# Two experts on each side of a convolution, run batch by batch, with the convolution's tiles put between the expert steps

## The chip, the cores and the metric

The kernel runs on one core of a Trainium2 chip. The metric is the device time of one execution in microseconds (us). The kernel before takes 614.93 us, the median of three runs (614.17 to 615.29). The engines are TensorE (PE in the rows, with its weight loads as PEld), VectorE (DVE), ScalarE (ACT), GpSimd (POOL) and SyncE (SP), whose queue issues all the DMAs here.

## The reference

The input x has 2 batches, 8 channels and 256 x 256 values. Four residual layers follow, each on a group-normalised input. Layers 0, 2 and 3 are expert layers, in which every channel has its own two-layer network. Layer 1 is a 3x3 convolution over all 8 channels, with binarised weights and copied edges.

```python
# _gn: mean and variance over 2 channels x 256 x 256, for each batch and each of 4 groups
x = x + _L0_conv_ref(_gn(x), ...)   # expert: h = gelu(x @ w1[e] + b1[e]); out = h @ w2[e] + b2[e]
x = x + _L1_conv_ref(_gn(x), weight, bias)   # conv 3x3, 8 -> 8 channels, weights sign(w) * mean|w|
x = x + _L2_conv_ref(_gn(x), ...)   # expert, as L0
x = x + _L3_conv_ref(_gn(x), ...)   # expert, exact gelu
```

w1 is 8 x 256 x 1024 and w2 is 8 x 1024 x 256, so an expert is 256 -> 1024 -> 256 for 2 x 256 tokens.

## The kernel before, in words

The 24 experts are numbered E0 to E23; E0 to E7 are layer 0, E8 to E15 layer 2, E16 to E23 layer 3. The convolution stands between E7 and E8.

**An expert step.** Every product is made of three matmuls (low part of the weights by high part of the data, high by low, high by high). One of the 8 steps t of an expert makes 128 of its 1024 hidden values: `g1` (L1004) issues 6 matmuls into a bank G1, ScalarE applies gelu and makes the high part (`gelu`, L559 and L563), VectorE subtracts for the low part (`h_lo`, L720), and two steps later `g2` (L1020) issues 6 matmuls that add to the two ACC banks. After the last step VectorE adds ACC, bias and residual into XT (`evict`, L734). A step is 512 columns wide when both batches run together. An expert in `HALVED` (E7, E8, E9) runs as two passes of 8 steps of 256 columns, one for each batch; E8 and E9 run in the order E8 batch 0, E9 batch 0, E8 batch 1, E9 batch 1. Beside the steps, ScalarE and VectorE split the next expert's weights into high and low parts (`w_hi`, `w_lo`, one of 8 pieces a step), and normalise and split its input (`norm`, `x_hi`, `x_lo`).

**The group statistics.** A job J is a chain over engines: `sums` (two bn_stats, VectorE), `aggregate`, `mean_over_partitions` (TensorE), `deviate`, `variance_over_partitions` (TensorE), `add_eps`, `rstd` (GpSimd), `scale_shift`. Then `norm`, `x_hi` and `x_lo` make an expert's input from it.

**The convolution.** XT has image rows on the partitions of each channel. The convolution wants all 8 channels of 16 rows on the partitions (XC), so each finished channel is stored to a DRAM scratch (`store_x1`) and loaded again (`load_xc`). A batch is 19 blocks of rows, in 10 tiles: nine of 512 columns and one of 256. Of each tile q, GpSimd normalises (`normalise_tile`, CN), ScalarE makes the high part Ch (L617), VectorE the low part Cl (`conv_low`, L894), TensorE issues 3 matmuls by Ch and 3 by Cl (L1122), ScalarE scales and adds the bias in the bank (L622), and VectorE adds into XC (`conv_add`, L903). Then `give_back` (L436) issues 20 DMAs a batch that bring XC back to XT. The semaphore `x2_in[b]` counts them.

**What sets the order.** Each engine's program is written out by hand and waits in order on semaphores. In the kernel before, TensorE finishes E7 (`drain`), then runs all 20 tiles, then E8. VectorE does the sums of batch 0 for E8 (job 9) after `conv_low` of tile 17, behind a wait for all 20 DMAs of batch 0:

```python
            conv_low(q - 3)
            dve.wait_ge(x2_in[0], 16 * pieces_back())
            sums(9, 0)
            sums_done(9)
            aggregate(9)
            conv_add(q - 5)
```

Of the kernel before, what the change touches and what calls it, by code (L numbers as in the profile page):

```python
# [108 lines left out]
def evicts_for(E, b, layer):


    if not isinstance(E, int):
# [5 lines left out]
    return evicts(E) - DC if E == C + 2 else evicts(E - 1)

ONE_BATCH = {7: 0, 8: 1, 9: 0, 10: 1}


def batches(J):

    return (ONE_BATCH[J],) if isinstance(J, int) and J in ONE_BATCH else tuple(range(B))


def jobs_weighed(J, late):

    return B * J - sum(J > j for j in ONE_BATCH) if isinstance(J, int) else B * J - (len(ONE_BATCH) if late else 0)

USUAL = dict(sums=0, aggregate=1, mean=3, deviate=3, variance=5, eps=6, scale=7)


def jobs_of(P, ee, f):


    if not isinstance(P, int):
        if f == 0:
            return [(2 * P + ee, USUAL, 2 * P - 2 if ee else 2 * P + 2, P - 1 if ee else NPAIR)]  # L150
        return [] if ee else [(P + 7, USUAL, 2 * (P - NPAIR * f) + 2, NPAIR)]
    E = 2 * P + ee
    if E == 0:
        return [(1, dict(sums=4, aggregate=5, mean=7, deviate=7), 2, NPAIR)]
    if E == 1:
        return [(1, dict(variance=0, eps=0, scale=1), 2, NPAIR)]
    if E == 7:
        return [(6, dict(sums=0, aggregate=1, mean=4, deviate=4, variance=6, eps=7, scale=8), 4, 2),
                (7, dict(sums=10, aggregate=11, mean=12, deviate=12, variance=13, eps=13, scale=14), 6, 3)]
    if E == C:  # L160
        return [(11, dict(mean=9, deviate=9, variance=11, eps=11, scale=12), 2, NPAIR)]
    if E == C + 1:
        return [(10, dict(sums=0, aggregate=0, mean=2, deviate=2, variance=3, eps=4, scale=4), 0, NPAIR),
                (11, dict(sums=5, more_sums=6, aggregate=7), 2, NPAIR)]
    if P >= 5 and ee == 0 and P + 1 < LAYERS * NPAIR:
        return [(P + 7, USUAL, (2 * P + 2) % C, NPAIR)]
    return []
# [29 lines left out]
def split_at(P, ee, t):

    E = 2 * P + ee
    if isinstance(P, int):  # L200
        if E == LAYERS * C - 1:
            return None
        if E == C:
            return t + 4 if t < 4 else None
        if E == C + 1:
            return t - HT if t >= HT else None
    return t if t < HT else None
# [955 lines left out]
```

## Time and profile before

| What | Value |
|---|---|
| median of three runs | 614.93 us |
| the profiled execution's own time | 614.43 us |
| its span, first to last instruction | 612.4 us |
| TensorE busy | 594.5 us (97%) |
| ScalarE busy | 430.3 us (70%) |
| VectorE busy | 423.2 us (69%) |
| GpSimd busy | 31.3 us (5%) |
| mean granted TensorE clock | 0.989 |

The rows further down come from this one execution. Times in them count from the span's start; the execution's own time is 2.0 us above the span. A busy TensorE is not TensorE at its peak, since matmuls overlap: the distance between the starts of two rows says more than the duration in one.

### The profile page before, as it was taken

How to read it: one execution, taken by the hardware profiler on the slowest of the kernel's cores; microseconds unless marked ns; L12 is line 12 of the kernel's file. 1: busy time of each engine (PE TensorE's matmuls, PEld its weight loads, DVE VectorE, ACT ScalarE, POOL GpSimd, SP SyncE). 2: the span in 40 equal slices, each digit the busy share in tenths (PEclk: the TensorE clock that was granted, in tenths of full speed). 3: DMA queues.
4: the chain of work that ended last, by engine and by line, in shares of the span. 5: the costliest groups of instructions: out<-in, count | busy, mean ns of one | idle time of the engine just before them, and what ended most of it. 6: DMA issues, size and time to landing. Idle time of an engine off the chain costs nothing.

```text
span 612.4 us, 9520 instructions
## 1 busy us (share of the span) xinstructions
PE 594.5 (97%) x2973; PEld 501.0 (82%) x2973; DVE 423.2 (69%) x857; ACT 430.3 (70%) x741; POOL 31.3 (5%) x52
## 2 busy tenths in 40 slices
PE   7999999999999896999999999999999999999997
PEld 7778888888889775999888888888888888888885
DVE  4867968768787796767865866866775675675532
ACT  5766767677777685769867777777767777777743
POOL 2000000000000451000000000000000000000000
PEclk9999999999999997999999999999999999999999
DMA  8673355455363599801332323223234244234001
GB/s 273 188 238 105 113 163 176 119 165 152 108 178 103 197 116 110 177 2 63 109 105 77 130 68 118 88 74 133 70 109 132 86 123 136 86 116 142 17 19 69
DMA packets 56342, 72.80 MB, mean 119 GB/s; under 512 B 4064, under 2 KB 50160, under 8 KB 56304
## 3 DMA queue, kind: packets, MB, share of 16 engines
q1 hardware_dynamic: 56304, 72.33, 41.5%
q8 instruction: 19, 0.31, 0.2%
q14 instruction: 19, 0.16, 0.1%
HBM read 59.70 MB, written 8.42 MB: 111 GB/s over the span
## 4 chain that ended last, share of the span: by engine, by line
PE 87%; DVE 4%; DMA 2%; issue 2%; SPq 2%; POOL 1%; ACT 1%; DVEq 0%; POOLq 0%; ACTq 0%
PE G L1016 42%; PE ACC L1039 14%; PE ACC L1034 14%; PE ACC L1035 14%; DMA W2raw<-in_L_conv_w 1%; DVE Cl L894 1%; DMA XT<-XC 1%; PE TR L1052 1%; SPq L374 1%; DVE XC L903 1%; DVE BN L653 1%; SPq L436 1%; PE ACC L1122 1%; PE TR L982 1%; PE STAT L995 0%
## 5 line engine op out<-in xcount | busy, mean ns | idle before, releaser
L720 DVE TENSOR_TENSOR Hl<-HR,Hh 128x512 fp32r<-128x512 f32 (+1 forms) x216 | 136.2, 631 | 158.8 <-ACT Hh L563 157.5
L559 ACT ACTIVATE HR<-G,BT 128x512 f32<-128x512 f32 (+1 forms) x216 | 138.3, 640 | 137.1 <-PE G L1016 135.9
L1016 PE MATMUL G<-Xh,W1l 128*128 128x512 f32 (+1 forms) x432 | 163.9, 379 | 3.3 <-issue 1.9
L1016 PE MATMUL G<-Xl,W1h 128*128 128x512 f32 (+1 forms) x432 | 158.7, 367 | 0.0
L1016 PE MATMUL G<-Xh,W1h 128*128 128x512 f32 (+1 forms) x432 | 158.5, 367 | 0.0
L1034 PE MATMUL ACC<-Hh,W2l 128*128 128x512 f32 (+1 forms) x432 | 156.5, 367 | 0.0
L1035 PE MATMUL ACC<-Hh,W2h 128*128 128x512 f32 (+1 forms) x432 | 156.2, 366 | 0.0
L563 ACT ACTIVATE Hh<-HR 128x512 fp32r<-128x512 f32 (+1 forms) x216 | 126.3, 585 | 8.7
L1039 PE MATMUL ACC<-Hl,W2h 128*128 128x512 f32 (+1 forms) x432 | 123.5, 367 | 0.6 <-DVE Hl L720 0.6
L1016 PEld LDWEIGHTS G<-Xh,W1l 128*128 128x128 f32 x432 | 82.0, 190 | 16.1 <-issue 2.2
L1016 PEld LDWEIGHTS G<-Xh,W1h 128*128 128x128 f32 x432 | 81.9, 189 | 13.6
L1034 PEld LDWEIGHTS ACC<-Hh,W2l 128*128 128x128 f32 x432 | 81.8, 189 | 13.4
L1035 PEld LDWEIGHTS ACC<-Hh,W2h 128*128 128x128 f32 x432 | 81.8, 189 | 13.2
L1016 PEld LDWEIGHTS G<-Xl,W1h 128*128 128x128 f32 x432 | 82.1, 190 | 11.5
L1039 PEld LDWEIGHTS ACC<-Hl,W2h 128*128 128x128 f32 x432 | 78.2, 189 | 14.5 <-DVE Hl L720 1.3
L699 DVE TENSOR_TENSOR W2l<-W2raw,W2h 128x512 fp32r<-128x512 f32 x96 | 65.6, 686 | 4.2 <-ACT W2h L546 3.6
L699 DVE TENSOR_TENSOR W1l<-W1raw,W1h 128x512 fp32r<-128x512 f32 x96 | 65.5, 686 | 2.7 <-ACT W1h L546 2.5
L546 ACT ACTIVATE W2h<-W2raw 128x512 fp32r<-128x512 f32 x96 | 58.9, 616 | 3.6 <-DMA W2raw<-in_L_conv_w 3.6
L546 ACT ACTIVATE W1h<-W1raw 128x512 fp32r<-128x512 f32 x96 | 58.6, 617 | 2.1 <-DMA W1raw<-in_L_conv_w 2.1
L653 DVE BATCH_NORM_STATS2 BN<-XT 128x6 f32<-128x512 f32 (+1 forms) x60 | 37.3, 680 | 3.2 <-DMA XT<-XC 3.2
L493 POOL TENSOR_TENSOR RS<-VE,half 128x2 f32<-128x2 f32 (+1 forms) x18 | 12.8, 708 | 489.4 <-DVE VE L677 489.4
L714 DVE TENSOR_TENSOR Xl<-XN,Xh 128x512 fp32r<-128x512 f32 x48 | 32.9, 686 | 0.6 <-ACT Xh L553 0.4
(73 smaller groups left out, 357.4 us busy)
## 6 DMA issues: line engine op xcount, KB each, us to landing
W1raw<-in_L_conv_w SPq DMA_DIRECT2D x24, 1024.0 KB, 5.1
W2raw<-in_L_conv_w SPq DMA_DIRECT2D x24, 1024.0 KB, 5.6
x_scratch<-XT SPq DMA_DIRECT2D x16, 256.0 KB
out_x<-OUTT SPq DMA_DIRECT2D x16, 256.0 KB, 2.2
XC<-x_scratch SPq DMA_DIRECT2D x16, 252.0 KB
XT<-XC SPq DMA_DIRECT2D x34, 112.0 KB
NAT<-in_x SPq DMA_DIRECT2D x6, 512.0 KB, 8.4
NAT<-in_x SPq DMA_DIRECT2D x4, 256.0 KB, 3.6
```

Of the source, the lines that this page charges most:

```text
L493: nc.gpsimd.tensor_tensor(RS[:, bs], VE[:, bs], half[:, bs], ALU.pow).then_inc(rs_done, 1)
L546: nc.scalar.activation(dst, src, ACT.Copy).then_inc(whi, 1)
L559: nc.scalar.activation(HR[:, t % 2, 0:n], G1[t % 2][:, 0:n], func, bias=BT[:, bass.ds(col, 1)]).then_inc(gelu_done, 1)
L563: nc.scalar.activation(Hh[:, t % RING, 0:n], HR[:, t % 2, 0:n], ACT.Copy).then_inc(hhi, 1)
L653: nc.vector.bn_stats(BN[:, b, i], at).then_inc(bn_done, 1)
L699: nc.vector.tensor_tensor(dst, src, high.bitcast(F32), ALU.subtract).then_inc(wlo, 1)
L714: nc.vector.tensor_tensor(Xl[:, par, :, b], XN[:, b], Xh[:, par, :, b].bitcast(F32), ALU.subtract).then_inc(xlo, 1)
L720: nc.vector.tensor_tensor(Hl[:, t % RING, 0:n], HR[:, t % 2, 0:n], Hh[:, t % RING, 0:n].bitcast(F32), ALU.subtract).then_inc(hlo, 1)
L1016: ins = nc.tensor.matmul(G1[t % 2][:, 0:width(b)], w[:, ee, c, col], rhs, start=n == 0, stop=n == len(parts) - 1)
L1034: nc.tensor.matmul(banks[m][:, 0:n], W2l[:, ee, t8, col], high, start=t8 == 0, stop=False)
L1035: nc.tensor.matmul(banks[m][:, 0:n], W2h[:, ee, t8, col], high, start=False, stop=False)
L1039: ins = nc.tensor.matmul(banks[m][:, 0:n], W2h[:, ee, t8, col], Hl[:, t % RING, 0:n], start=False, stop=t8 == HT - 1)
```

## The change

The experts that run batch by batch are now E6, E7, E8 and E9, `CROSSED`, in the order of a list of passes. P6 to P9 are E6 batch 0, E7 batch 0, E6 batch 1, E7 batch 1; P10 to P13 are E8 batch 0, E9 batch 0, E8 batch 1, E9 batch 1. A unit u is a step t of a pass, and tables say at which unit everything stands. The tiles of the convolution of batch 0 (0 to 9) stand in TensorE's program from P8 step 7 to P9 step 4, those of batch 1 (10 to 19) from P10 step 4 to P11 step 1. TensorE finishes P9 before it begins P10, and P11 before P12. The loops are written out, HR has 4 buffers in place of 2 and lies under Hl, CN lies under Cl with 3 buffers, and the copied edges of XC (`double_edges`) move from VectorE to GpSimd. In a tile, ScalarE no longer scales the bank: it adds the bias to XC, and VectorE's `conv_add` multiplies the bank by the mean weight and adds.

```diff
-HALVED = (C - 1, C, C + 1)
-CROSSED = (C, C + 1)
+BOTH = tuple(range(B))
+CROSSED = (C - 2, C - 1, C, C + 1)
+PASSES = ([(E, BOTH) for E in range(C - 2)]
+          + [(E, (b,)) for pair in (CROSSED[0:2], CROSSED[2:4]) for b in range(B) for E in pair]
+          + [(E, BOTH) for E in range(C + 2, EXPERTS)])
...
+EARLY = (6, TILES)
+CONV_AT = {unit(P8, 7): (0,), unit(P9, 0): (1, 2, 3), unit(P9, 1): (4, 5), unit(P9, 3): (6, 7, 8), unit(P9, 4): (9,),
+           unit(P10, 4): (10,), unit(P10, 5): (11, 12), unit(P10, 6): (13,), unit(P10, 7): (14, 15),
+           unit(P11, 0): (16, 17), unit(P11, 1): (18, 19)}
...
+    (0, (0,), 0.5, dict(sums=unit(P9, 7), aggregate=unit(P9, 7), mean=unit(P9, 7), variance=unit(P9, 7),
+                        eps=unit(P9, 7), scale=unit(P9, 7))),
...
+            for e in (C - 2, C - 1):
+                store_x1(e, (0,), x1_last[e - C + 2][0])
+                load_xc(e, (0,), x1_last[e - C + 2][0], 48, xc_last[0])
+            for q in range(TILES):
+                give_back(q)
+            store_x1(C - 2, (1,), x1_last[0][1])
+            load_xc(C - 2, (1,), x1_last[0][1], 48, xc_last[1])
+            load_w1(C + 1)
+            store_x1(C - 1, (1,), x1_last[1][1])
+            load_xc(C - 1, (1,), x1_last[1][1], 48, xc_last[1])
+            load_w2(C + 1)
...
+            def conv_high(q):
...
+                nc.scalar.activation(Ch[:, q % CRING, 0:w], CN[:, q % CRING, 0:w], ACT.Copy
+                                     ).then_inc(chi, 1)
+                at = XC[:, b, own, 1:N + 1]
+                nc.scalar.activation(at, at, ACT.Identity, bias=conv_bias[:, 0:1]).then_inc(cbiased, 1)
...
+                if u in (unit(P9, 7), unit(P11, 7)):
+                    evict(p)
...
+                if u == unit(P9, 7):
+                    norm(P10, 0)
+                    x_lo(P10, 0)
...
+                waits_for_conv = p in (P10, P12)
+                tiles = CONV_AT.get(u, ())
+                if waits_for_conv and t == 0:
+                    g2(u - 2)
+                    g2(u - 1)
+                    for J in jobs_at("mean", u - 1):
+                        mean_over_partitions(J)
+                        variance_over_partitions(J)
+                g1(u)
+                for q in tiles[0:1]:
+                    conv_tile(q)
+                if u >= 2 and not (waits_for_conv and t < 2):
+                    g2(u - 2)
+                for q in tiles[1:]:
+                    conv_tile(q)
```

In the kernel before, TensorE's rows at the end of E7 (L1034 to L1039 are `g2`) go straight over into tiles 0 and 1 (BAND), and nothing but tiles and two statistics matmuls follows until E8:

```order
L1034 MATMUL ACC_1<-Hh,W2l 128x256
L1035 MATMUL ACC_1<-Hh,W2h 128x256
L1039 MATMUL ACC_0<-Hl,W2h 128x256
L1039 MATMUL ACC_1<-Hl,W2h 128x256
L1122 MATMUL ACC_0<-Ch,BAND 128x512 x3
L1122 MATMUL ACC_0<-Cl,BAND 128x512 x3
L1122 MATMUL ACC_1<-Ch,BAND 128x512 x3
L1122 MATMUL ACC_1<-Cl,BAND 128x512 x3
```

Now, in P9 step 0 of TensorE's program, tile 1 stands between the end of a `g1` (L959) and a whole `g2` (L976 to L981), and tiles 2 and 3 behind it:

```order
L959 MATMUL G_0<-Xh,W1h 128x256
L995 MATMUL ACC_1<-Ch,BAND 128x512 x3
L995 MATMUL ACC_1<-Cl,BAND 128x512 x3
L976 MATMUL ACC_0<-Hh,W2l 128x256
L977 MATMUL ACC_0<-Hh,W2h 128x256
L976 MATMUL ACC_1<-Hh,W2l 128x256
L977 MATMUL ACC_1<-Hh,W2h 128x256
L981 MATMUL ACC_0<-Hl,W2h 128x256
L981 MATMUL ACC_1<-Hl,W2h 128x256
L995 MATMUL TR<-Ch,BAND 128x512 x3
```

So the tiles have moved among the steps of P8 to P11. At the place where E8 batch 0 begins, TensorE's program before has the last two tiles (of batch 1) around the variance matmul (STAT<-Q) of E8's input, and then the first `g1` of E8:

```order
L1122 MATMUL ACC_0<-Ch,BAND 128x512 x3
L1122 MATMUL ACC_0<-Cl,BAND 128x512 x3
L1001 MATMUL STAT<-Q,ones_mean 128x1
L1122 MATMUL ACC_1<-Ch,BAND 128x256 x3
L1122 MATMUL ACC_1<-Cl,BAND 128x256 x3
L1016 MATMUL G_0<-Xh,W1l 128x256
```

Now the last `g2` of P9 stands there, the mean and the variance matmul directly behind it, and the first `g1` of P10 behind them:

```order
L977 MATMUL ACC_1<-Hh,W2h 128x256
L981 MATMUL ACC_0<-Hl,W2h 128x256
L981 MATMUL ACC_1<-Hl,W2h 128x256
L938 MATMUL STAT<-MV,ones_mean 128x1
L944 MATMUL STAT<-Q,ones_mean 128x1
L959 MATMUL G_0<-Xh,W1l 128x256
```

So at this place no tile is left between the statistics and E8. VectorE's program at the same place (P9 step 7) now reads as follows; what a row waits for stands in brackets, XT<-ACC is `evict`, BN to ST is the statistics job, XN and Xl are `norm` and `x_lo`:

```order
L737 TENSOR_TENSOR Hl<-HR,Hh 128x256 [waits hhi]
L752 SCALAR_TENSOR_TENSOR XT<-ACC_0,BT,XT 128x256 [waits g2_done]
L752 SCALAR_TENSOR_TENSOR XT<-ACC_1,BT,XT 128x256
L673 BN_STATS BN<-XT 128x6 [waits x2_in0] x2
L679 BN_AGGR MV<-BN 128x2 [waits bn_done]
L685 COPY MEAN<-STAT 128x1 [waits mean_mm]
L689 SCALAR_TENSOR_TENSOR Q<-DM,MV 128x1 [waits dm_done]
L695 TENSOR_SCALAR VE<-STAT 128x1 [waits var_mm]
L702 COPY ST<-RS 128x1 [waits rs_done]
L725 TENSOR_SCALAR XN<-XT,ST 128x2x256 [waits g1_done,st_done]
L731 TENSOR_TENSOR Xl<-XN,Xh 128x2x256 [waits xhi]
```

Before, `conv_low` and `conv_add` rows of tiles 15 to 19 stood between these rows (from which the `evict` was absent); now they stand in one run behind the `evict` of E7 batch 1. P11 step 7 has the same rows for batch 1.

## Rows read from the trace of the kernel before

**Rows 1.** The page, busy time, share of the span, instructions of TensorE

```profile
PE 594.5 (97%) x2973; PEld 501.0 (82%) x2973; DVE 423.2 (69%) x857; ACT 430.3 (70%) x741; POOL 31.3 (5%) x52
```

**Rows 2.** Timeline of TensorE (start, us, what), end of E7 to E8

```profile
202.70 0.40 PE L1039 MATMUL ACC<-Hl,W2h 128*128 128x256 f32 x2
204.40 0.94 PE L1122 MATMUL ACC<-Ch,BAND 128*128 128x512 f32 x3 [1.30 <-ACT Ch L617]
...
225.42 0.87 PE L1122 MATMUL ACC<-Cl,BAND 128*128 128x512 f32 x3
226.13 0.87 PE L1122 MATMUL ACC<-Ch,BAND 128*128 128x512 f32 x3
...
235.68 0.58 PE L995 MATMUL STAT<-MV,ones_mean 128*128 128x1 f32 x2 [3.72 <-DVE MV L660]
236.13 1.63 PE L1122 MATMUL ACC<-Ch,BAND 128*128 128x512 f32 x3
...
238.84 0.42 PE L1001 MATMUL STAT<-Q,ones_mean 128*128 128x1 f32 x2
...
242.79 0.36 PE L1016 MATMUL G<-Xh,W1l 128*128 128x256 f32 x1 [1.95 <-issue]
```

**Rows 3.** Windows of 1 us: busy of PE, PEld, DVE, ACT, POOL, PEclk, DMA share, GB/s

```profile
236.00:237.00 1.00, 1.00 (x4) 0.90 (x4) 0.96 (x5) 0.00 (x0) 0.00 (x0) 0.50 1.06 98
...
245.00:246.00 1.00, 1.00 (x7) 1.00 (x6) 1.00 (x3) 0.97 (x3) 0.00 (x0) 0.50 1.03 130
```

**Rows 4.** Timeline of the DMA queue (SP), return of XC to XT

```profile
211.64 34.07 SPq L436 DMA_DIRECT2D XT<-XC  x40
```

**Rows 5.** Chain that ended last, in order of time: the last return of batch 0

```profile
227.72 6.36 DMA XT<-XC
```

**Rows 6.** Timeline of TensorE in E7: first row of two steps in succession

```profile
181.65 0.28 PE L1016 MATMUL G<-Xh,W1l 128*128 128x256 f32 x1
...
183.09 0.28 PE L1016 MATMUL G<-Xh,W1l 128*128 128x256 f32 x1
```

**Rows 7.** Chain in order of time in E6: `g1` of two full steps

```profile
165.30 1.36 PE G L1016 x6
...
168.02 1.36 PE G L1016 x6
```

**Rows 8.** Timeline of TensorE early in E8: two matmuls at the lower clock

```profile
245.06 0.41 PE L1016 MATMUL G<-Xh,W1h 128*128 128x256 f32 x1
245.27 0.41 PE L1016 MATMUL G<-Xh,W1l 128*128 128x256 f32 x1
```

**Rows 9.** Timeline of VectorE: start of job 0; E7 batch 0's evict; E8's input

```profile
8.06 0.28 DVE L660 BATCH_NORM_AGGREGATE MV<-BN 128x2 f32<-128x12 f32 x2
...
193.20 0.87 DVE L734 SCALAR_TENSOR_TENSOR XT<-ACC,BT,XT 128x256 f32<-128x256 f32 x2
...
234.10 1.29 DVE L653 BATCH_NORM_STATS2 BN<-XT 128x6 f32<-128x512 f32 x2 [3.16 <-DMA XT<-XC]
...
239.29 0.16 DVE L677 TENSOR_SCALAR VE<-STAT 128x1 f32<-128x1 f32 x1 [1.52 <-PE STAT L1001]
```

**Rows 10.** Timeline of TensorE: the variance matmul of job 0

```profile
9.48 0.38 PE L1001 MATMUL STAT<-Q,ones_mean 128*128 128x2 f32 x2
```

**Rows 11.** Timeline of ScalarE at E8's input

```profile
240.89 0.54 ACT L622 ACTIVATE ACC<-ACC,conv_bias,conv_mean 128x256 f32<-128x256 f32 x1 [1.06 <-PE ACC L1122]
241.35 0.62 ACT L553 ACTIVATE Xh<-XN 128x512 fp32r<-128x512 f32 x1
```

**Rows 12.** Groups by line and shape, ScalarE: busy us, mean ns

```profile
L559 ACT ACTIVATE HR<-G,BT 128x256 f32<-128x256 f32 x48 | 22.6, 471 | 15.5 <-PE G L1016 15.0 <-DVE Hl L720 0.5
...
L563 ACT ACTIVATE Hh<-HR 128x256 fp32r<-128x256 f32 x48 | 20.0, 418 | 1.5
...
L622 ACT ACTIVATE ACC<-ACC,conv_bias,conv_mean 128x512 f32<-128x512 f32 x18 | 13.3, 738 | 6.3 <-PE ACC L1122 6.3
...
L617 ACT ACTIVATE Ch<-CN 128x516 fp32r<-128x516 f32 x18 | 11.4, 633 | 7.8 <-POOL CN L499 7.2
```

More of the change, by code:

```diff
@@ new lines, in last_pass, with unit, halved, width @@
+def last_pass(E):
+    return pass_of(E, B - 1)
+def unit(p, t):
+    return HT * p + t
+def halved(p):
+    return len(PASSES[p][1]) == 1
+def width(p):
+    return N * len(PASSES[p][1])
+SPLITS = [(p, b) for p, (E, bs) in enumerate(PASSES) for b in bs]
+def split_no(p, b):
+    return SPLITS.index((p, b))
+def evicted_by(p):
+    return DC * (p + 1)
+P6, P7, P8, P9, P10, P11, P12, P13 = (pass_of(E, b) for pair in (CROSSED[0:2], CROSSED[2:4])
+                                      for b in range(B) for E in pair)
@@ new lines, in split_steps, with weight_steps @@
+def split_steps():
+    at = {}
+    for p, b in SPLITS[2:]:
+        if p in (P6, P7):
+            at[unit(p - 1, 2)] = (p, b)
+        elif p == P8:
+            at[unit(P6, 5)] = (p, b)
+        elif p == P9:
+            at[unit(P7, 5)] = (p, b)
+        elif p == P11:
+            at[unit(P10, 4)] = (p, b)
+        elif p == P13:
+            at[unit(P12, 4)] = (p, b)
+        elif p not in (P10, P12):
+            at[unit(p - 1, 2 + 2 * b)] = (p, b)
+    return at
+def weight_steps():
+    at = {}
+    for E in range(1, EXPERTS):
+        p = first_pass(E) - 1
+        steps = [unit(p, t) for t in range(HT)]
+        if E == C:
+            steps = [unit(P9, t) for t in (4, 5, 6, 7)] + [unit(P10, t) for t in (0, 1, 2, 3)]
+        elif E == C + 1:
+            steps = [unit(P10, t) for t in (4, 5, 6, 7)] + [unit(P11, t) for t in (1, 3, 5, 7)]
+        for k, u in enumerate(steps):
+            at.setdefault(u, []).append((E, k))
+    return at
@@ new lines, with jobs_at, job_of, weighed @@
+NJOBS = len(JOBS)
+CONV_JOBS = {b: [J for J, (e, bs, of, _) in enumerate(JOBS) if of == 0 and b in bs] for b in range(B)}
+LAST_CONV_JOB = {b: max(CONV_JOBS[b]) for b in range(B)}
+def jobs_at(stage, u):
+    return [J for J, job in enumerate(JOBS) if job[3].get(stage) == u]
+def job_of(E, b):
+    f, e = divmod(E, C)
+    of = (-1, 0.5, 1)[f]
+    return next(J for J, job in enumerate(JOBS) if job[2] == of and job[0] == e - e % 2 and b in job[1])
+def weighed(J):
+    return sum(len(job[1]) for job in JOBS[:J])
@@ L126 @@
[L126 to L167, printed above, removed]
@@ L197, in split_at, with blocks, tile_width @@
[L197 to L207, printed above, removed]
+PIECES_BACK = sum(len(rows_back(k)) for k in range(NBLK))
+def blocks(q):
+    b, i = divmod(q, TILES)
+    return b, slice(2 * i, min(2 * i + 2, NBLK))
+def tile_width(q):
+    b, own = blocks(q)
+    return own.stop - own.start
```

889 lines of the change are left out of this document (387 added, 502 removed).

## The prediction

> **What bounds the kernel now.** I read the page first: TensorE is busy for 97% of the span and the other engines for about 70% or less [rows 1]. So a change can gain only where TensorE stands still, runs at the lower clock, or has work that it need not have. Everything here happens in one region, so I then read TensorE's timeline there. E7's last `g2` pair starts at 202.70 and ends at 203.10; E8's first `g1` starts at 242.79 [rows 2]. That is 39.7 us for 20 tiles. A group of 3 matmuls starts 0.71 us after the one before [rows 2], so a tile of 512 columns is 1.41 us; a tile of 256 columns is 6 matmuls at 0.12 us, the distance of the 256-wide matmuls (1.44 us for a step of 12 [rows 6]). 18 x 1.41 + 2 x 0.72 = 26.8 us. The phase wastes 39.7 - 26.8 = 12.9 us. The reader sees three of its waits in brackets: 1.30 for the first Ch, 3.72 and 1.95 us, the last two for the input of E8 [rows 2]. Part of the rest is the clock: at 236 us it is granted at 0.50, which is 1.2 of 2.4 GHz, after the wait of 3.72 us [rows 3], and the tile begun at 236.13 takes 2.71 us up to the variance matmul at 238.84, where 1.41 is usual [rows 2].
>
> After the last wait the clock falls once more, in E8's steps: 0.50 at 245 us [rows 3], where matmuls start 0.21 us apart and not 0.12 [rows 8]. About 15 matmuls run so (the timeline there has them from 244.5 to 247.6), 15 x 0.09 = 1.4 us. So the region costs 41.1 us, of which 14.3 is waste. That is the most that the change can win.
>
> **Why E8 waits in the kernel before.** Batch 0's statistics need every row of XC back in XT. SP issues 40 returns in 34.07 us, from 211.64 on [rows 4]; the last of batch 0 is issued at 227.72 and takes 6.36 us to land, at 234.08 [rows 5]. bn_stats starts at 234.10, after 3.16 us of waiting [rows 9]. From first issue to last landing, batch 0's return takes 22.4 us, and the 16 DMA engines are full at about 100 to 130 GB/s meanwhile [rows 3].
>
> **The change, part by part.**
>
> *Tiles among the steps.* Their 26.8 us of TensorE work stay. What goes is the 14.3 us of waste, if nothing takes its place. Batch 0's tiles stand between P8 step 7 and P9 step 4. From the first `conv_add`, at the beginning of P9, to the end of P9 lie 8 steps (11.5 us), 9 tiles (8 x 1.41 + 0.72 = 12.0 us) and the two last `g2` (half a step each, 1.4 us): 25 us. The return wants 22.4 us from its first issue, so it is just covered, with 2 to 3 us to spare, and costs nothing. If that cover were gone, each us of lateness would be a us of TensorE's time. Batch 1's return has the rest of P10 and P11, about the same, with W2 of E9 (1 MB) ahead of it in the queue; also covered, since six steps (8.6 us) follow its last tile.
>
> *The first tile.* It needs E7 batch 0 stored and loaded again. Before, the evict of E7 batch 0 starts at 193.20 and ends at 194.07 [rows 9], and the first tile runs at 204.40 [rows 2]: 10.3 us. Now that evict stands in P8 step 2, and the tile behind the `g1` of P8 step 7. That is 5.5 steps or 7.9 us after the beginning of step 2, where the evict needs 0.9 us. So TensorE waits 0.9 + 10.3 - 7.9 = 3.3 us at most. In the old path the copied edges stood in VectorE's queue behind `h_lo`, and CN and Ch may be some 1.7 us quicker now. I take 2.0 (bounds 1.0 and 3.3; nothing excludes less if the loads had landed much before).
>
> *The boundary at P10.* This is the dear part. TensorE has nothing to run between the last `g2` of P9 and the first `g1` of P10, but the two statistics matmuls. VectorE has the evict of P9 ahead of the sums. The chain: evict 0.04 + 0.87 [rows 9]; two bn_stats 1.29 [rows 9]; from the start of bn_aggr at 8.06 [rows 9] to the end of the variance matmul at 9.86 [rows 10] 1.80 us for two batches, less 0.2 for one batch, 1.6; `add_eps` 0.2; from its start at 239.29 to `g1` at 242.79 [rows 2, 9] 3.5 us, less its own 0.16 and less 0.3 for which Xh stood behind an L622 [rows 11], 3.0. Sum 7.0 us. Before, the same chain ran from 234.08 to 242.79 beside two tiles of batch 1. Now it is bare.
>
> *The boundary at P12* has the same rows for batch 1: 7.0 us again. Before, batch 1's input was made during E9 batch 0, at no cost. So there are two bare chains, 14.0 us.
>
> *The clock at the boundaries.* After the wait of 3.72 us, what ran at 1.2 GHz cost 1.3 us in the one tile above, and the short tile behind it, at 0.21 in place of 0.12 us a matmul [rows 6, 8], 6 x 0.09 = 0.5; after the 1.95 us, another 1.4 us. So a wait costs 1.4 (one such stretch) to 3.2 us (both). I take 2.0 a boundary, 4.0 in all. The Trainium skill, "TensorE: Matmul & The Clock Gate", section "HAM oscillation — how this bites in real kernels", speaks against the change here: a wait between bursts of matmuls that is repeated makes each next burst begin cold, every time. By it, both boundaries pay; the row at 0.50 agrees for the wait that the trace has.
>
> *E6 in two passes.* A full step is 2.72 us [rows 7], two half steps 2 x 1.44 = 2.88 [rows 6]: 8 x 0.16 = 1.3 us. The same page, section "Back-to-back issue gap", gives a warm gap of N / 2.4 + 2.5 ns, 109 for 256 columns and 216 for 512, by which halving costs 0.03 us a step and some 0.2 in all; the rows have 120 ns, and they decide.
>
> *ScalarE beside the tiles.* A tile costs it 0.63 + 0.74 = 1.37 us, a half step 0.47 + 0.42 = 0.89 [rows 12]. From P10 step 4 to P11 step 1: 10 x 1.37 + 6 x 0.89, and 4 weight pieces at about the price of Ch, 21.5 us, where TensorE has 12.0 + 1.4 + 6 x 1.44 = 22.0. There is no slack, and in-order waits on GpSimd's CN come on top; bounds 0 and 4 us, I take 1.0 for both groups of tiles. P6, which must now split E7's weights in half the time, is as tight (8 x 1.5 in 11.5 us); I put it into the bound.
>
> *The rest.* Written-out loops, deeper HR, edges on GpSimd, one finer wait in `g2` for the weights: they lie where TensorE waits for nothing, and I cost them at nothing; TensorE's steps follow each other at 2.72 us there [rows 7]. Two statistics matmuls of 0.3 us leave the phase of the tiles and come back among steps, +0.3.
>
> **Sum.** After: 26.8 + 2.0 + 14.0 + 4.0 + 1.3 + 1.0 + 0.3 = 49.4. Before: 41.1. Difference +8.3. The profiled execution took 614.43 us in all, so 622.7; it lies 0.5 below the median of the runs, and I say 623.0.
>
> **The rivals.**
>
> *The returns are late.* SP issues in order. The store and load of E6 batch 1 stand behind all ten returns of batch 0, and those of E7 batch 1 behind a wait for E8's W1. If the DMA engines, full in [rows 3], need longer than 25 us for the return or if the loads of batch 1's XC miss P10 step 4, each us is added. For it: the path has 10.3 us when the queue is empty, and it now shares with a 1 MB load; margins are 2 to 3 us. Against: batch 0's return took 22.4 us including its gaps. It gives 3 to 7 us more, 626 to 630.
>
> *It is faster.* The mechanism is the one that the change lays out: all waste of the phase is hidden, and the boundary is shorter than my chain. It decides at the point where two boundaries with their clock cost less than 14.3 - 2.0 - 1.3 - 1.3 = 9.7 us, 4.85 each. The chain of ten links alone gives 7.0, and I find no link that could run early, since VectorE's program has the evict first. If it came out at 3.5 us each with no fall of the clock, the time would be 612. For it speaks only that the prices of the middle links come from job 0.
>
> *The clock stays up or the chain is 1 us shorter.* TensorE's clock stayed at full in the wait of 1.30 us before 204.40. If each boundary costs 5.5 in place of 9.0 us, the sum is +1.3: 616.
>
> **How the numbers follow.** Forecast with its own range 618 to 628: 0.72. Late returns: 0.12. Short boundaries, 615.5 to 618: 0.07. The shorter boundaries of the second rival: 0.09. Within 0.2% of the kernel before (about what a measurement can tell from no change, 613.7 to 616.2) lie 0.03 of the short boundaries and 0.01 of the second rival. The range from 617 to 629 leaves about 2 in 10 out. Faster 0.08, same 0.04, slower 0.88.
>
> **What the profile after would show.** TensorE idle before the first `g1` of P10 and of P12, about 7 us each, released by Xl, with two statistics matmuls in the middle and a clock of 0.50 behind; an idle of about 2 us before the first Ch matmul; half steps of 1.44 us in E6; bn_stats of both batches not waiting for XT<-XC. I am wrong if bn_stats waits for the DMA (late returns), if the time between `g2` and `g1` at P10 is under 5 us, or if the tiles come much more than 1.41 us apart beside the steps (ScalarE as the bound).

## The result, and the profile after

| | before | after |
|---|---|---|
| median | 614.74 us (614.17 to 615.29) | 646.67 us (645.75 to 647.97, 4 runs) |
| span of the profiled execution | 612.4 us | 646.2 us |
| mean granted TensorE clock | 0.989 | 0.973 |

The ratio is 1.052, 95% interval 1.0497 to 1.0546. The change costs 31.9 us. The prediction had the sign, and said +8.3.

The page of the changed kernel, busy time, share of the span and instructions (the view of [rows 1]), and the granted clock in 40 slices:

```profile
PE 608.9 (94%) x3069; PEld 514.1 (80%) x3069; DVE 427.2 (66%) x869; ACT 431.1 (67%) x757; POOL 32.8 (5%) x56
...
PEclk9999999999998957897999999999999999999999
```

TensorE's share falls from 97% to 94%; the share of no other engine rises. In us TensorE stands idle for 37.3 in place of 17.9, and its rows cover 14.4 us more (608.9 for 594.5). Little of that is new work (the 96 more matmuls are those of E6's halves, 1.3 us by the prediction's rows); the rest is rows that run longer, at the slow clock and in another place of memory (below).

**Where it lies.** E6 to E10 is the region that the change touches. From E6's first `g1` to E10's first it takes 136.15 us before (154.26 to 290.41), and 164.44 after (155.64 to 320.08): 28.3 of the 31.9 us. The rest is outside it, which the prediction had not looked at: E6 begins 1.4 us later, and from E10 to the end it takes 326.1 us and not 322.0. Experiment 1 accounts for this rest.

**The boundary at P10**, TensorE's timeline (the view of [rows 2]; in brackets the idle time before a row and what released it):

```profile
223.66 0.40 PE L981 MATMUL ACC<-Hl,W2h 128*128 128x256 f32 x2
226.47 0.38 PE L938 MATMUL STAT<-MV,ones_mean 128*128 128x1 f32 x2 [2.41 <-DVE MV L679]
227.42 0.38 PE L944 MATMUL STAT<-Q,ones_mean 128*128 128x1 f32 x2 [0.57 <-DVE Q L689]
230.97 0.55 PE L959 MATMUL G<-Xh,W1l 128*128 128x256 f32 x1 [3.16 <-issue]
```

and VectorE's there (the view of [rows 9]):

```profile
224.10 0.88 DVE L752 SCALAR_TENSOR_TENSOR XT<-ACC,BT,XT 128x256 f32<-128x256 f32 x2
224.90 1.28 DVE L673 BATCH_NORM_STATS2 BN<-XT 128x6 f32<-128x512 f32 x2
...
228.93 0.55 DVE L725 TENSOR_SCALAR XN<-XT,ST 128x512 f32<-128x512 f32 x1
230.17 0.69 DVE L731 TENSOR_TENSOR Xl<-XN,Xh 128x512 fp32r<-128x512 f32 x1 [0.70 <-ACT Xh L575]
```

From the end of the last `g2` (223.66 + 0.40 = 224.06) to `g1` it is 6.9 us, and the two bn_stats have no wait for a DMA in front of them. The boundary at P12 has the same rows from 289.28 to 296.17, 6.9 us. The bare chains are as predicted, and the returns are in time.

**Between the boundaries** TensorE's timeline shows what was not predicted. These are all its waits above 0.7 us between `g1` of P8 step 7 and P12, but for the two boundaries:

```profile
194.62 1.42 PE L995 MATMUL ACC<-Ch,BAND 128*128 128x512 f32 x3 [2.65 <-issue]
236.28 0.58 PE L938 MATMUL STAT<-MV,ones_mean 128*128 128x1 f32 x2 [2.42 <-DVE MV L679]
244.14 0.97 PE L995 MATMUL ACC<-Ch,BAND 128*128 128x512 f32 x3 [0.73 <-ACT Ch L598]
248.20 1.65 PE L995 MATMUL ACC<-Cl,BAND 128*128 128x512 f32 x3 [3.09 <-DVE Cl L801]
265.26 0.36 PE L959 MATMUL G<-Xh,W1l 128*128 128x256 f32 x1 [2.02 <-DVE W1l L716]
279.60 0.36 PE L976 MATMUL ACC<-Hh,W2l 128*128 128x256 f32 x1 [0.94 <-DVE W2l L716]
283.60 0.36 PE L976 MATMUL ACC<-Hh,W2l 128*128 128x256 f32 x1 [0.93 <-DVE W2l L716]
287.62 0.36 PE L976 MATMUL ACC<-Hh,W2l 128*128 128x256 f32 x1 [1.64 <-DVE W2l L716]
```

The first is the first tile, 2.65 us (predicted 2.0). The others, 11.8 us, are in P10 and P11, where I had put 1.0 us for all. Two of them are read from VectorE and ScalarE together. VectorE in P10:

```profile
234.71 1.28 DVE L673 BATCH_NORM_STATS2 BN<-XT 128x6 f32<-128x512 f32 x2
236.02 0.21 DVE L679 BATCH_NORM_AGGREGATE MV<-BN 128x2 f32<-128x12 f32 x1
...
242.20 0.16 DVE L764 TENSOR_REDUCE CST<-of_group 128x2 f32<-128x8 f32 x1
...
246.39 0.69 DVE L716 TENSOR_TENSOR W2l<-W2raw,W2h 128x512 fp32r<-128x512 f32 x1 [3.62 <-ACT W2h L570]
247.00 0.54 DVE L725 TENSOR_SCALAR XN<-XT,ST 128x512 f32<-128x512 f32 x1
247.45 1.30 DVE L801 TENSOR_TENSOR Cl<-CN,Ch 128x516 fp32r<-128x516 f32 x2
```

Job 9, the convolution's statistics of batch 1, begins only at 234.71, behind the `h_lo` and `w_lo` of P10 step 0, though its data have lain in XT since P9's evict. TensorE waits 2.42 us for it at its mean matmul. Later VectorE stands for 3.62 us at a W2l piece of which nothing is urgent, and Cl of tile 10 is queued behind it. ScalarE tells why:

```profile
243.46 0.63 ACT L598 ACTIVATE Ch<-CN 128x516 fp32r<-128x516 f32 x1 [1.15 <-POOL CN L532]
244.00 0.71 ACT L601 ACTIVATE XC<-XC,conv_bias 128x512 f32<-128x512 f32 x1
244.61 0.62 ACT L598 ACTIVATE Ch<-CN 128x516 fp32r<-128x516 f32 x1
245.13 0.71 ACT L601 ACTIVATE XC<-XC,conv_bias 128x512 f32<-128x512 f32 x1
245.74 0.61 ACT L570 ACTIVATE W2h<-W2raw 128x512 fp32r<-128x512 f32 x1
```

The piece W2h (245.74) stands behind the first two Ch, and these wait for CN, which waits for job 9.

**The clock** in windows of 1 us (columns as in [rows 3]) is 0.50, that is 1.2 of 2.4 GHz, for two long stretches of P10: from 229 us, in the boundary, to 242, with the wait of 2.42 us inside, and again from 246, in the wait of 3.09 us, to 252.

```profile
232.00:233.00 1.00, 1.00 (x6) 1.00 (x6) 0.00 (x0) 0.38 (x1) 0.00 (x0) 0.50 0.01 3
...
240.00:241.00 1.00, 1.00 (x6) 1.00 (x6) 0.63 (x2) 0.00 (x0) 0.29 (x1) 0.50 0.00 0
...
250.00:251.00 1.00, 1.00 (x7) 1.00 (x6) 1.00 (x3) 0.03 (x1) 0.94 (x1) 0.50 1.08 386
```

**A full step** is 2.76 us and not 2.72 [rows 7]. The chain of the changed kernel, `g1` of two successive full steps (the view of [rows 7]):

```profile
386.18 1.38 PE G L959 x6
388.94 1.37 PE G L959 x6
```

The half steps of E7 (the view of [rows 6]) are 1.41 to 1.43 us, where they were 1.44; they have become a little shorter:

```profile
182.30 0.70 PE G L959 x6
183.71 0.71 PE G L959 x6
```

### The profile page after: what moved, and what is told of

Same layout as the page of the kernel before. It is cut to its first block, busy times and chain, and to the rows that moved or that the text cites. A ratio compares the mean times of both kernels' runs of the same rounds, so it can differ in the third digit from the quotient of the medians.

```text
span 646.2 us, 8775 instructions
## 1 busy us (share of the span) xinstructions
PE 608.9 (94%) x3069; PEld 514.1 (80%) x3069; DVE 427.2 (66%) x869; ACT 431.1 (67%) x757; POOL 32.8 (5%) x56
## 4 chain that ended last, share of the span: by engine, by line
PE 83%; issue 4%; DVE 4%; ACT 4%; DMA 3%; POOL 1%; SPq 0%; DVEq 0%; ACTq 0%; POOLq 0%
PE G L959 38%; PE ACC L976 13%; PE ACC L981 13%; PE ACC L977 13%; PE ACC L995 3%; DMA W1raw<-in_L_conv_w 2%; DMA W2raw<-in_L_conv_w 1%; DVE BN L673 1%; ACT HR L585 1%; PE TR L1008 1%; PE TR L995 1%; ACT W2h L570 1%; ACT W1h L570 1%; DVE W1l L716 1%; PE TR L925 1%
## 5 line engine op out<-in xcount | busy, mean ns | idle before, releaser
L959 PE MATMUL G<-Xh,W1l 128*128 128x512 f32 (+1 forms) x448 | 168.6, 376 | 9.4 <-issue 6.3
L976 PE MATMUL ACC<-Hh,W2l 128*128 128x512 f32 (+1 forms) x448 | 161.9, 367 | 4.1 <-DVE W2l L716 3.5
L959 PE MATMUL G<-Xh,W1h 128*128 128x512 f32 (+1 forms) x448 | 163.6, 365 | 0.0
L959 PE MATMUL G<-Xl,W1h 128*128 128x512 f32 (+1 forms) x448 | 163.3, 365 | 0.0
L981 PE MATMUL ACC<-Hl,W2h 128*128 128x512 f32 (+1 forms) x448 | 127.6, 366 | 1.0 <-DVE Hl L737 1.0
L959 PEld LDWEIGHTS G<-Xh,W1l 128*128 128x128 f32 x448 | 86.8, 194 | 22.7 <-issue 8.9
L976 PEld LDWEIGHTS ACC<-Hh,W2l 128*128 128x128 f32 x448 | 85.8, 192 | 19.1 <-issue 5.0
L959 PEld LDWEIGHTS G<-Xh,W1h 128*128 128x128 f32 x448 | 86.5, 193 | 13.3
L959 PEld LDWEIGHTS G<-Xl,W1h 128*128 128x128 f32 x448 | 86.9, 194 | 12.0
L981 PEld LDWEIGHTS ACC<-Hl,W2h 128*128 128x128 f32 x448 | 80.8, 191 | 16.0 <-DVE Hl L737 1.6
L575 ACT ACTIVATE Xh<-XN 128x512 fp32r<-128x512 f32 x48 | 29.7, 620 | 18.0 <-DVE XN L725 17.9
L673 DVE BATCH_NORM_STATS2 BN<-XT 128x6 f32<-128x512 f32 x60 | 37.2, 679 | 0.0
```

Of the source, the lines that this page charges most:

```text
L575: nc.scalar.activation(Xh[:, par, :, b], XN[:, par, :, b], ACT.Copy).then_inc(xhi, 1)
L673: nc.vector.bn_stats(BN[:, J % 2, b, i], XT[:, :, b, e + i]).then_inc(bn_done, 1)
L959: ins = nc.tensor.matmul(G1[u % 2][:, 0:n], w[:, par, c, col], rhs, start=i == 0, stop=i == len(parts) - 1)
L976: nc.tensor.matmul(acc(p, m), W2l[:, par, t, col], high, start=t == 0, stop=False)
L981: ins = nc.tensor.matmul(acc(p, m), W2h[:, par, t, col], low, start=False, stop=t == HT - 1)
```

## The experiments

All ratios are to the kernel before, timed beside each run on the same chip. Its median was 614.21 us beside `lay1536`, `j9`, `w9` and `clk`, 615.43 beside `before_pad`, `q10`, `sum4` and `nob12`, and 614.35 beside the others. The changed kernel was not timed again beside them (its 646.67 us stand beside 614.74), so "below the changed kernel" can be off by about 1 us.

The runs of one kernel also scatter by up to 4.1 us, and the traces show two places for it that no edit touches: the first tile, behind whose wait the clock falls in some traces and not in others (1.5 us, see the last section), and the end (from the first `g1` of E23 it takes 31.3 us in `sum4` and 32.9 in `sum5`, with the same program there). So beside each median I read one stretch that lies between these two, **the stretch from P9 to E10**: from P9's first `g1` to E10's first. In the changed kernel it takes 121.7 us (198.35 to 320.08). It is one execution of each kernel, but free of the two.

**1. Where Hh and Hl lie.** The new buffers move the start of Hh and Hl in each partition, from 1536 to 1920 bytes past a multiple of 2048 (added up from the sizes of the buffers ahead of them). `lay1536` puts them back in the changed kernel:

```diff
+        PAD = sb("PAD", [PART, 416])
         with ExitStack() as use:
             HR = sb("HR", [PART, RING, TOK], F32, use)
```

Expected: 

> The changed kernel with 1,664 unused bytes a partition ahead of HR and Hl, so that Hh and Hl begin at the same offset within 2,048 bytes as before (1536 and not 1920). Nothing else differs. Address theory: the full steps of the changed kernel start 2.75 to 2.77 us apart and not 2.72 (an expert of layer 2 takes 22.13 us and not 21.76) because of where Hh, Hl and Xl now lie; then the experts E10 to E23 fall back by 0.3 us each and the time by some 5 us, to 641. Rival (the written-out loops, or HR in the memory of Hl): the step stays at 2.76 and the time at 646.7, within 1 us.

Measured: 642.47 us (641.55 to 643.15), ratio 1.0461 (1.0438 to 1.0483), 4.2 us below the changed kernel. `before_pad` does the reverse to the kernel before.

Expected: 

> The kernel before with 384 bytes of unused buffer ahead of HR, so that Hh and Hl begin 1920 bytes past a multiple of 2048 in each partition, as in the changed kernel, and not 1536. Nothing else is changed. Address theory (the 2.72 us of a full step become 2.75 to 2.77 us because of where Hh and Hl lie): the 168 full steps lose about 0.03 us each, 614.5 becomes 618 to 620. Rival (the 0.03 us come from the written-out program or from the finer wait in g2, and the 1536-byte run of the changed kernel won by chance): no change, 613.7 to 615.7.

Measured: 619.90 us (619.73 to 620.33), ratio 1.0081 (1.0055 to 1.0107): +4.5 us. The chain of `lay1536`, two full steps:

```profile
385.08 1.36 PE G L960 x6
387.80 1.36 PE G L960 x6
```

and that of `before_pad`:

```profile
382.82 1.38 PE G L1017 x6
385.58 1.38 PE G L1017 x6
```

Both ways the place of the buffers alone makes a full step 2.72 or 2.76 us. In the groups by shape the matmul of W2l by Hh takes 396 ns in `before_pad` (390 in the kernel before) and 389 in `lay1536` (396 in the changed kernel):

```profile
L1035 PE MATMUL ACC<-Hh,W2l 128*128 128x512 f32 x336 | 132.9, 396 | 0.0
```

```profile
L977 PE MATMUL ACC<-Hh,W2l 128*128 128x512 f32 x320 | 124.6, 389 | 0.0
```

This is also nearly all of the loss outside the region. From E10 to the end `lay1536` takes 321.5 us and `before_pad` 325.9, where the kernel before takes 322.0 and the changed kernel 326.1. The half steps go the other way: the eight of E9 before E10 take 11.36 us in the changed kernel and in `before_pad`, and 11.52 in `lay1536` and in the kernel before. So `lay1536` is 0.5 us longer in the stretch from P9 to E10 (122.2), and gains outside it.

Two more places in the kernel before, `before_0` (a multiple of 2048) and `before_1024`, ask whether another place would gain.

Expected (`before_0`): 

> The kernel before with Hh and Hl at a multiple of 2048 bytes in each partition (512 bytes of unused buffer ahead of HR), in place of 1536 past it. If only the offset 1920 is bad, the time is that of before within 1 us. If the offset matters by the distance to a multiple of 2048, or of a larger power, it may lie on either side: a full step's spacing of 0.2267 us a matmul is above 512 columns / 2.4 GHz = 0.2133, so up to 0.16 us a step are there to be had, and 0.03 us more or less in a step is 5 us in all.

Expected (`before_1024`): 

> The kernel before with Hh and Hl 1024 bytes past a multiple of 2048 (1536 bytes of unused buffer ahead of HR). As for the offset 0: equal to before within 1 us if 1920 is a bad place among good ones; if some offset removes the slow W2l matmuls and the rest of the 0.2267 us as well, faster by up to 27 us, of which I expect nothing.

Measured: 614.49 us, ratio 1.0001 (0.9991 to 1.0010), and 614.60 us, ratio 1.0002 (0.9990 to 1.0013). So of four places three are equal and 1920 is bad. Why, the runs don't tell.

**2. Job 9 earlier** (`j9`): its sums and aggregate go behind `x_lo(P10, 0)`, into P9 step 7.

```diff
-    (6, (1,), 0, dict(sums=unit(P10, 0), aggregate=unit(P10, 0), mean=unit(P10, 1), ...
+    (6, (1,), 0, dict(mean=unit(P10, 1), ...
...
                     norm(P10, 0)
                     x_lo(P10, 0)
+                    sums(9)
+                    aggregate(9)
```

Expected: 

> The two bn_stats and the aggregate of job 9 (batch 1 of the convolution's input) move from P10 step 0 on VectorE to the end of P9 step 7, behind x_lo of P10, where VectorE had nothing to do for 2.7 us. Theory of the queues: TensorE's wait of 2.42 us for that aggregate goes, CST is ready some 2 to 3 us sooner, and so is the first tile of batch 1, whose wait of 3.09 us for Cl shrinks: 3 to 6 us less in all, 641 to 644. Theory of the clock (TensorE at 1.2 GHz from 228 to 243 us is what costs, and the waits merely stand in it): under 1.5 us less, since the stretch at the lower clock stays.

Measured: 643.84 us (642.31 to 645.82), ratio 1.048 (1.0454 to 1.0505), 2.8 us below the changed kernel; its runs reach into those of the changed kernel. The stretch from P9 to E10 takes 120.1 us, 1.7 less. In TensorE's timeline the wait at the mean matmul is gone, but tile 10 now waits longer for Ch, and as long as before for Cl:

```profile
242.54 0.98 PE L997 MATMUL ACC<-Ch,BAND 128*128 128x512 f32 x3 [2.75 <-ACT Ch L598]
246.60 1.65 PE L997 MATMUL ACC<-Cl,BAND 128*128 128x512 f32 x3 [3.07 <-DVE Cl L801]
```

The slow clock behind the boundary ends sooner too, so P10's first four steps take 7.4 us in place of 11.5, but the next one takes 10.4 in place of 8.5. So the chain job 9, CST, CN, Ch is late as a whole, and what is taken from its start partly comes back at its end.

**3. E9's W2 pieces earlier** (`w9`). `g2` now waits for each pair of steps' W2l, where it waited for the whole of E9's weights before it began.

```diff
-            steps = [unit(P10, t) for t in (4, 5, 6, 7)] + [unit(P11, t) for t in (1, 3, 5, 7)]
+            steps = [unit(P10, t) for t in (4, 5, 6, 7)] + [unit(P11, t) for t in (1, 2, 4, 6)]
```

Expected: 

> The last three of the four W2 pieces of E9 are split one step earlier (P11 steps 1, 2, 4, 6 in place of 1, 3, 5, 7). Theory of the queues: g2 of P11 waits for them three times (0.94, 0.93 and 1.64 us) since each is split in the step before the one that needs it; one step more is enough and 3 to 3.5 us go, 643.4. Rival: ScalarE and VectorE have no room there, the waits return as later gelu or evict, and under 1 us goes.

Measured: 644.29 us (642.82 to 646.93), ratio 1.0487 (1.046 to 1.0515); the median is 2.4 us lower, though the runs overlap those of the changed kernel. In the trace the three waits of 0.94, 0.93 and 1.64 us become one:

```profile
284.35 0.36 PE L976 MATMUL ACC<-Hh,W2l 128*128 128x256 f32 x1 [0.22 <-DVE W2l L716]
```

and E6 to E10 takes 161.3 in place of 164.4 us, 3.0 of it in the stretch from P9 to E10 (118.7). Only the placing of the pieces was changed, so the three waits come from it.

**4. The weight piece ahead of the first Ch** (`q10`), on ScalarE. The code is that of every step, but only P10 step 3 has both a weight piece and a first Ch:

```diff
-                if u in FIRST_TILES:
-                    for q in (FIRST_TILES[u], FIRST_TILES[u] + 1):
-                        conv_high(q)
                 if E == 0 and t in (0, 2):
                     x_evac(4 + t)
                 for weight in WEIGHTS_AT.get(u, ()):
                     w_hi(*weight)
+                if u in FIRST_TILES:
+                    for q in (FIRST_TILES[u], FIRST_TILES[u] + 1):
+                        conv_high(q)
```

Expected: 

> The changed kernel with one thing moved on ScalarE: in P10 step 3 the last weight piece of E8 stands ahead of the two first Ch of batch 1 and not behind them. Theory of the queues (the 3.09 us for Cl of tile 10 come from VectorE, whose w_lo and norm stand ahead of conv_low(10) and wait for this piece): the wait falls to below 0.7 us, and the time by about 2.5 to 3 us, 643.5 to 644.5. Rival (the statistics of job 9 are late, and whatever stands behind CST waits all the same): the wait for the first Ch stays at about 0.7 and what is won at Cl comes back before the g1 of P11 (2.02 us now), so less than 1 us in all.

Measured: 642.61 us (642.09 to 642.96), ratio 1.045 (1.0423 to 1.0477): 4.1 us below the changed kernel, more than either theory said. The wait for Cl is 0.38 us and not 3.09, and the one before P11's `g1` falls as well:

```profile
243.21 0.97 PE L995 MATMUL ACC<-Ch,BAND 128*128 128x512 f32 x3 [0.94 <-ACT Ch L598]
244.56 0.97 PE L995 MATMUL ACC<-Cl,BAND 128*128 128x512 f32 x3 [0.38 <-DVE Cl L801]
...
260.22 0.36 PE L959 MATMUL G<-Xh,W1l 128*128 128x256 f32 x1 [1.45 <-DVE W1l L716]
```

The rival falls: nothing came back. In this trace the clock also did not fall at the first tile (from `g1` of P8 step 7 to the next it takes 5.7 us, and 7.25 in the changed kernel), which lies ahead of everything that the edit touches. But the stretch from P9 to E10, behind that tile, takes 117.4 us, 4.4 less, so the 4.1 us of the medians need not come from the first tile. Of the 4.4 us, 1.6 are in P11's first two steps (7.85 for 9.41 us), where the clock stays at 1.00 behind the wait of 1.45 us and fell behind the one of 2.02. It stayed up there in `clk` too, behind 1.99 us, so this part may be chance. The other 2.8 us are what the theory of the queues expected.

**5. Are the causes separate?** `sum4` has edits 1 to 4 together.

Expected: 

> Four edits together: Hh and Hl at 1536 bytes past a multiple of 2048, job 9's sums in the boundary of P9, E9's W2 pieces at P11 steps 1, 2, 4, 6, and the weight piece of P10 step 3 ahead of the first Ch. Alone the first three gave 4.2, 2.8 and 2.4 us. If the four causes are separate: 646.7 - 4.2 - 2.8 - 2.4 - 2.8 = 634.5. If they hide one another (a wait taken away comes back at the next), 637 to 640. What is left over 623 then belongs to the boundaries and to ScalarE beside the tiles.

Measured: 633.08 us (631.67 to 635.42), ratio 1.0306 (1.0273 to 1.0339), 13.6 us below the changed kernel. The four alone gave 4.2 + 2.8 + 2.4 + 4.1 = 13.5. They add, and not by the luck of the first tile: the stretch from P9 to E10 takes 112.8 us, 8.9 less than in the changed kernel, and the four alone changed it by +0.5 - 1.7 - 3.0 - 4.4 = -8.6. Two waits are left in P10 and P11 beside the boundaries:

```profile
239.42 1.03 PE L998 MATMUL ACC<-Ch,BAND 128*128 128x512 f32 x3 [2.62 <-ACT Ch L599]
256.92 0.35 PE L962 MATMUL G<-Xh,W1l 128*128 128x256 f32 x1 [2.22 <-DVE W1l L717]
```

ScalarE's timeline has the last W1 piece behind a Ch that waits for GpSimd:

```profile
254.28 0.63 ACT L599 ACTIVATE Ch<-CN 128x516 fp32r<-128x516 f32 x1 [0.99 <-POOL CN L533]
254.82 0.71 ACT L602 ACTIVATE XC<-XC,conv_bias 128x512 f32<-128x512 f32 x1
255.43 0.61 ACT L571 ACTIVATE W1h<-W1raw 128x512 fp32r<-128x512 f32 x1
```

`sum5` is `sum4` with these pieces one step earlier:

```diff
-            steps = [unit(P10, t) for t in (4, 5, 6, 7)] + [unit(P11, t) for t in (1, 2, 4, 6)]
+            steps = [unit(P10, t) for t in (3, 4, 5, 6)] + [unit(P11, t) for t in (1, 2, 4, 6)]
```

Expected: 

> The run with four edits plus a fifth: E9's W1 pieces at P10 steps 3, 4, 5, 6 and not 4, 5, 6, 7, on ScalarE and VectorE. Theory of the queues (the 2.22 us before the first g1 of P11 are the last piece, which stands on ScalarE behind a Ch that waits for GpSimd's CN, and the slow matmuls behind it): 633.1 falls by 2.5 to 3.8 us, to 629.3 to 630.6. Rival (the engines beside the tiles are simply full, and a piece earlier makes the tiles later by as much): within 1 us of 633.1.

Measured: 629.56 us (628.62 to 630.26), ratio 1.0241 (1.0226 to 1.0257), another 3.5 us; the stretch from P9 to E10 takes 108.9 us, another 3.9. The wait of 2.22 us is gone, and the slow clock behind it too: 255 to 260 us is granted at 0.72 in `sum4` and at 1.00 in `sum5`. What is left at P10 is the first tile of batch 1:

```profile
240.64 1.33 PE L998 MATMUL ACC<-Ch,BAND 128*128 128x512 f32 x3 [3.12 <-ACT Ch L599]
241.77 1.48 PE L998 MATMUL ACC<-Cl,BAND 128*128 128x512 f32 x3
```

**6. The price of the clock.** `clk` puts 24 matmuls without use into each boundary, so that TensorE is not idle there.

```diff
                     for J in jobs_at("mean", u - 1):
+                        keep_clock(9)
                         mean_over_partitions(J)
+                        keep_clock(2)
                         variance_over_partitions(J)
+                        keep_clock(13)
```

Expected: 

> At both boundaries (P9 to P10, P11 to P12) TensorE runs 24 small matmuls on constants into the free bank TR between the statistics matmuls: 9 before the mean, 2 before the variance, 13 before g1. They add nothing to the result. Theory of the clock: TensorE stays at 2.4 GHz into P10 and P12; the half steps at 1.2 GHz (0.21 us a matmul from 231.0 to 242.4 and from 296.2 to 300.6) become 0.12, and together with what follows them 5 to 8 us go: 639 to 642. Theory of the queues: the matmuls are faster, but TensorE then waits longer for the same late CST, Cl and weights in P10, and 2 to 3.5 us go, most of it at P12.

Measured: 645.45 us (644.78 to 647.19), ratio 1.0517 (1.0488 to 1.0546), not told apart from the changed kernel's 646.67, and less than either theory said. The edit does keep the clock: the window from 228 to 232 us is granted at 1.00, where it was 0.62. But at P10 step 1 TensorE then waits 2.99 us for job 9 and not 2.42, and 1.59 for Ch and not 0.73. So this run can't price the clock. `sum5clk` puts the same matmuls into `sum5`, where the wait at job 9's mean is gone (that of tile 10 is not).

Expected: 

> The run with five edits plus the 24 matmuls without use in each boundary, which keep the clock at full there. In the changed kernel alone they gained 1.2 us. If that was little because late queues waited anyway for what a faster clock gave, now that these waits are gone they gain the 4.0 us that the prediction's clock term has for both boundaries (3 to 4.5). If the clock behind a boundary costs little in itself, 0.5 to 1.5 us.

Measured: 628.16 us (626.46 to 628.90), 1.4 us below `sum5` in the median, with runs that overlap (628.62 to 630.26). In the stretch from P9 to E10 the gain is 1.1 us (107.8 for 108.9). So keeping the clock through both boundaries gives 1.1 to 1.4 us, where I had 2.0 each. The traces show where the rest goes. At P12 the first three steps take 3.05 us in place of 4.78, 1.7 less, which is near my 2.0; then TensorE waits for VectorE, and of the 1.7 us 0.7 are left at E10:

```profile
286.71 0.50 PE L989 MATMUL ACC<-Hl,W2h 128*128 128x256 f32 x2 [1.00 <-DVE Hl L738]
```

At P10 the wait of tile 10 for Ch is 3.43 us in place of 3.12, and behind it 0.4 us are left. So the slow matmuls cost about what I took, but most of it overlaps with work that the other engines still have to do.

**7. The price of a boundary** (`nob12`). E8 batch 1 reads E8 batch 0's normalised input, so this part of the output is not the reference's, and TensorE need not wait at P12.

```diff
-                    pe.wait_ge(xlo, split_no(p, bs[-1]) + 1)
+                    pe.wait_ge(xlo, split_no(P10, 0) + 1 if p == P12 else split_no(p, bs[-1]) + 1)
...
-                waits_for_conv = p in (P10, P12)
+                waits_for_conv = p == P10
```

Expected: 

> The changed kernel without the boundary at P12. E8 batch 1 reads the normalised input of E8 batch 0 and not its own (this part of the output is not the reference's); the evict of P11 moves to P12 step 2 and job 10's matmuls, add_eps and scale_shift to P12 steps 0 and 1, still ahead of E9 batch 1. So TensorE has E8 batch 1 to run at once. Bare-chain theory (7.0 us of waits plus a slow clock behind): 646.7 falls by 7 to 9.5 us, to 637 to 640. Rival 1 (the clock costs nothing here): by 7.0 or a little less. Rival 2 (something else binds at this place, the returns or the evicts): by less than 4 us.

Measured: 638.97 us (637.89 to 639.21), ratio 1.0383 (1.0355 to 1.0411): 7.7 us below the changed kernel. The trace has it in the right place: from the `g1` of P11 step 7 to E10's first it takes 28.02 us (283.16 to 311.18), and 35.69 in the changed kernel (284.39 to 320.08), 7.7 less. The bare chain of 6.9 us is gone; the other 0.8 are a balance, of which the trace shows these parts. The wait for the last W2l piece is 0.94 us and was 1.64, and the clock stays at 1.00 in P12; against that the mean matmul now waits 0.40 us, and a wait of 0.87 us stands in P12:

```profile
295.23 0.39 PE L960 MATMUL G<-Xh,W1l 128*128 128x256 f32 x1 [0.87 <-ACT HR L585]
```

## Why the prediction was wrong

The sign was right and so was its mechanism: two bare chains, 7.0 us each predicted, 6.9 in the trace, and 7.7 less by the run without one of them. The returns were in time. The first tile waited 2.65 us, within its bounds of 1.0 to 3.3. bn_stats waits for no DMA. The size was wrong by 23.6 us (31.9 for 8.3), and the time lies 18 us above the range. By the prediction's own steps:

- **"The rest ... I cost them at nothing" failed.** It named TensorE's steps at 2.72 us as the proof that nothing waits there, which is true; but the same edit moved Hh and Hl, and the step itself became 2.76 us: 4.2 us (`lay1536`, and 4.5 in reverse). I had not asked what a deeper buffer does to the ones behind it. "One finer wait in `g2` for the weights" was costed at nothing too: with the new places of the W2 pieces it is three waits and 2.4 us (`w9`).
- **"ScalarE beside the tiles ... I take 1.0" (bounds 0 and 4) failed.** I had summed busy times over P10 and P11, 21.5 us against 22.0, and put "in-order waits ... on top" into the bound. The sum was not what decided. The order was: W2h behind the first Ch 4.1 us (`q10`; the trace lets 1.6 of them be chance), W1h behind a later Ch 3.5 us (`sum5` against `sum4`), and the sums of job 9 behind VectorE's steps 2.8 us (`j9`). None of these edits takes work away, and by the medians they give 10.4 us together.
- **A step that is missing: the first tile of batch 1.** I costed a wait for the first tile of batch 0 alone. Job 9 can only start once P9's evict is done, at the boundary, and its chain runs over four engines to CST, CN and Ch. Even in `sum5` tile 10 waits 3.12 us, and from the `g1` of P10 step 4 at 236.63 to the next at 244.33 it takes 7.70 us where a half step and a tile need 1.44 + 1.41. That is 4.9 us. The rival of late returns named the loads of batch 1's XC, not this chain; it was the wrong thing to be late.
- **The first tile of batch 0, 2.0**, was a wait without a clock behind it. From `g1` of P8 step 7 at 191.10 to the next at 198.35 it takes 7.25 us, less 2.85, 4.4. A term mis-sized by 2.4. In the three traces where the clock stays up there it is 5.7 to 5.8 us, so some 1.5 of the 2.4 are the clock.
- **"I take 2.0 a boundary, 4.0 in all" was too much** for the two boundaries: 1.4 (`sum5clk`). The step that failed is the overlap. I had priced the slow matmuls, between 1.4 us for one slow stretch of the kernel before and 3.2 for both, and they do cost that much (1.7 at P12); but VectorE's Hl and the late tile 10 take most of it back when the clock is kept. The page that I weighed there, the Trainium skill, "TensorE: Matmul & The Clock Gate", section "HAM oscillation — how this bites in real kernels", says that every burst after such a gap begins cold. At the two boundaries the traces agree: without the added matmuls the clock falls to 0.50 at each of them in every trace. At the first tile, behind 2.6 to 2.8 us, it fell in seven traces and not in three.

Together: 4.2 + 2.4 + 10.4 - 1.0 (what I had for ScalarE) + 4.9 + 2.4 - 2.6 = 20.7 of the 23.6 us. The first three (17.0; the way from 646.67 to 629.56 is 17.1) are shown by runs, each to about 1 us; the two first tiles are read from traces and weren't taken away in a run. 2.9 us stay open; the waits of 0.5 us for `cadded` before a `g2` of P9, which have their row in every trace here, are part of them.

No version of the change that was run comes near the kernel before: the best, `sum5clk`, is at 628.16 us, ratio 1.0219 (1.0200 to 1.0239), and what is left holds two bare chains of 7 us each and the two first tiles, 4.4 and 4.9 us. The change trades 14.3 us of waste for these 23, and that trade alone loses. Whether the tiles of batch 1 could stand later and save the 4.9 was not tried.

## What to carry to other kernels

When work is laid between the steps of an in-order program, the sum of busy times per engine doesn't price it. Walk each queue instead, and ask of every item that waits for another engine what stands behind it and who needs that: a weight piece without urgency, queued behind an item that waited, held up the tile behind it by 3.09 us here, and moving three lines of code left 0.38 of it. A chain of small operations over four engines, as group statistics are, costs its full length (7 us here) wherever nothing else is left for the engine that bounds, so count how many times a schedule lays it bare, for the first use of each batch as well. And after a change in buffers, compare the spacing of the matmuls in a part of the program that the change does not touch.
